# Two cross-attention layers on one core: the plain scores of the second layer read 48 rows each instead of 112

## The chip, the cores and the metric

One of the eight cores of a Trainium2 chip runs the whole program; the others are idle. The time is device microseconds from start to end of one execution, the median of three runs for the kernel before. Engines: TensorE (PE for matmuls, PEld for the loads of its stationary operand), VectorE (DVE), ScalarE (ACT), GpSimd (POOL), and SyncE (SP), which issues most DMAs.

## The reference

Sixteen batches, each with 112 query rows `x` of width 320 and 375 context rows of width 192, go through two attention layers. What matters here, for one batch:

```
# layer 0: 8 heads of width 40; keys are the first 371 context rows
hs  = softmax(q0 k0^T / sqrt(40)) v0            # plus a small attention over 4 extra tokens (ca_hs2)
x1  = (hs + ca_hs2) @ Wout + b_out + x
# layer 1: 20 heads of width 16; keys are all 375 context rows
q = (x1 @ Wq), k = (ctx @ Wk), v = (ctx @ Wv)
s = q k^T / sqrt(16)                            # per head: 112 x 375
out = softmax(s) v @ Wo + bo + x1
```

## The kernel before

Every float32 product that needs accuracy is made of float32r parts: an operand is split into a high part and a low remainder. For layer 1 a head has width 16, and its query is kept three times (high, low, high) in `q1T` and its key three times (low, high, high) in `k1_stack`, so that one contraction over 3 x 16 = 48 rows gives all three partial products. Two heads share a column block: the even head (j = 0) has its 48 rows at partitions 0 to 47, the odd head (j = 1) at partitions 64 to 111. `q1T[:, pair, j, :]` holds the query of head j and zeroes in the other head's rows (line 663 writes the even part, line 826 the odd part with its zeroes, through the factor `odd_rows`).

A softmax needs the row maximum before the exponent. So the scores are computed twice. `scores(g, pair)` computes the plain scores, queries on PSUM's partitions and 376 keys along the columns, for two heads at a time: head j goes to `bankS[:, j]`, which is a PSUM bank of its own. VectorE takes the negative maxima of both heads in one instruction (`maximum`, line 770). `transpose_m` (1162) transposes these maxima, VectorE copies them (776), and a DMA issued by ScalarE places them as a further row of the query (row 48). `shifted_scores` (1177, 1183) then computes the scores again, transposed, with the maximum subtracted, and `attend` (1215) multiplies their exponentials with the values. A group is four heads, so two pairs; layer 1 has five groups per batch, which makes ten pairs per batch and 160 pairs in all, each of two matmuls at line 1149. Layer 0 has its own line, 1146, and is not touched.

The matmuls of `attend`, of line 1115 and of line 987 write only 32 or 64 PSUM partitions each: they run in column tiles, parts of TensorE's array that are used side by side. In the set-up, the last two matmuls of each `query_keys` (line 971) contract over only 64 rows. A float32 matmul shows in the trace as two instructions, a float32r one as one.

The order of the work on each engine is written out by hand. A step t of the loop has seven slots; in a slot TensorE does: first pair of a group, units of phase 0, `shifted_scores` of an older group, `transpose_m`, units of phase 1, second pair, units of phase 2, `attend`, units of phase 3. The units (table `UNITS`) are all the projections and transposes; they share two PSUM banks in turn, so a unit waits until the unit two places before it has been drained by ScalarE or VectorE. Layer 1 is scored in slots 2 to 6. In steady state TensorE goes through the ten pairs of a batch as follows (units in brackets by their name in the table; most of them run at line 995):

- slot 2: [K1_0] **pair 1** [K1_1], shifted scores, maxima, [S3] **pair 2** [N1b, S2_0], attend, [S2_1]
- slot 3: **pair 3** [K1_2], shifted scores, maxima, [K0_0] **pair 4** [hn1T], attend, [K0_1]
- slot 4: **pair 5** [K0_2], shifted scores, maxima, [N0, p3T] **pair 6** [out1], attend, [q0T_0]
- slot 5: **pair 7** [hn0T, V0_0], shifted scores, maxima, [q0T_1] **pair 8** [out0], attend, [T2_0]
- slot 6: **pair 9** [x1T, V0_1], shifted scores, maxima, [T2_1] **pair 10** [q1], attend, [V0_2]

The units hn1T, hn0T, x1T (line 1077), N0, N1a, N1b (1085), q0T (1061) and T2 (1108) are float32 transposes; S3 is line 1123, S2 line 1101, p3T line 1088.

Of the kernel before, what the change touches and what calls it, by code (L numbers as in the profile page):

```python
# [11 lines left out]
B, SQ, HID = 16, 112, 320  # L12
SK, CAD, NTOK = 375, 192, 4
SKE = SK - NTOK
SKP = SK + 1
# [22 lines left out]
M_ROW0, M_ROW1 = 3 * D0, 3 * D1  # L38
ROWS1 = 64 + 3 * D1
# [53 lines left out]
def bank(name, b):  # L93
    return AT[name, b] % 2


def drained(name, b):
    return AT[name, b] // 2 + 1
# [13 lines left out]
def xattn_kernel(nc, xT, xpad, ctxT, caS, caT, w_all, w_ca, wqT, bd96, consts, bias, out):  # L112
    g_rows = nc.dram_tensor("g_rows", [B, 3, 32, HID], F32, kind="Internal").ap()

    with ExitStack() as ctx:
        def sb(name, shape, dt=F32):
            return ctx.enter_context(nc.sbuf_tensor(name, shape, dt))
# [14 lines left out]
        k1_stack = [sb(f"k1_stack{i}", [P, H1 // 2, SKP], F32R) for i in range(2)]  # L132
# [10 lines left out]
        q1T = sb("q1T", [P, H1 // 2, 2, SQ], F32R)  # L143
# [69 lines left out]
        bankS = ctx.enter_context(nc.psum_tensor("bankS", [P, 2, 512], F32))  # L213
# [729 lines left out]
        def _(pe):  # L943
# [183 lines left out]
            def scores(g, pair):  # L1127
                layer, b, k = g
                n = NUMBER[g]
                if n > 0 or pair > 0:  # L1130
                    pe.wait_ge(max_done, 2 * n + pair)
                else:
                    pe.wait_ge(gq_drained, 4)
                if pair == 0 and layer == 0:
                    if k == 0:
                        pe.wait_ge(k0_stacked, 16 * DMAS_K0 * (b + 1))
                    pe.wait_ge(bank_drained[bank(f"q0T_{k}", b)], drained(f"q0T_{k}", b))
                if pair == 0 and layer == 1:
                    if k == 0:
                        pe.wait_ge(k1_stacked[b % 2], 16 * DMAS_K1 * (b // 2 + 1))  # L1140
                        pe.wait_ge(k1_stacked_pool[b % 2], 16 * DMAS_K1 * (b // 2 + 1))
                    pe.wait_ge(bank_drained[bank(f"q1T_{k // 2}", b)], drained(f"q1T_{k // 2}", b))
                for j in range(2):
                    h = GROUP * k + 2 * pair + j
                    if layer == 0:
                        last = nc.tensor.matmul(bankS[0:SQ, j, 0:SKE + 1], q0T[0:M_ROW0, h, :],  # L1146
                                                k0_stack[0:M_ROW0, h, 0:SKE + 1], start=True, stop=True)
                    else:
                        last = nc.tensor.matmul(bankS[0:SQ, j, 0:SKP], q1T[0:ROWS1, h // 2, h % 2, :],  # L1149
                                                k1_stack[b % 2][0:ROWS1, h // 2, :], start=True, stop=True)  # L1150
                last.then_inc(scores_done, 1)

            def transpose_m(g, attended):
# [81 lines left out]
            for t in ITERATIONS:  # L1235
                for i in range(SLOTS):
                    g, before, late = scored_at(t, i), scored_at(t, i, 1), scored_at(t, i, LAG)
                    if g:
                        scores(g, 0)
                    for u in units_of(t, i, 0):  # L1240
                        unit(*u)
                    if late:
                        shifted_scores(late)
                    if before:
                        transpose_m(before, attended)
                        transposed = NUMBER[before] + 1
                    for u in units_of(t, i, 1):
                        unit(*u)
                    if g:
                        scores(g, 1)  # L1250
                    for u in units_of(t, i, 2):
                        unit(*u)
                    if late:
                        attend(late, transposed)
                        attended = NUMBER[late] + 1
                    for u in units_of(t, i, 3):
                        unit(*u)
# [75 lines left out]
```

## Time and profile before

| | |
|---|---|
| median of 3 runs | 777.53 us (777.09 to 777.82) |
| the profiled execution | 777.66 us, of which the span is 775.8 us |
| TensorE matmul busy | 713.3 us, 92% of the span |
| TensorE load busy | 615.3 us, 79% |
| VectorE, ScalarE, GpSimd busy | 61%, 51%, 38% |
| mean granted clock of TensorE | 0.98 of full speed |

Times are microseconds from the start of the span, unless marked ns. A row of the timeline begins with the start and the duration of an instruction or of a run of equal instructions (xN), then engine, source line, operation, the tiles written and read, and the shapes. Behind a matmul's names stand contraction rows * stationary columns, then the moving operand's size: `112*112 112x376` is a contraction of 112 rows, 112 stationary columns and 376 moving columns. A recorded matmul reaches beyond the start of the next one, because matmuls are pipelined and their ends are modelled; the distance from one start to the next is what TensorE spends. A bracket at the end gives idle time before the instruction and what ended it.

### The profile page before, as it was taken

The page shows a single profiled execution, that of the slowest core. Times are in us where ns is not written, and L with a number is a line of the kernel's source. Part 1 is how long each engine was busy: PE and PEld are TensorE (multiplying, and loading weights), DVE is VectorE, ACT ScalarE, POOL GpSimd, SP SyncE. Part 2 cuts the span into 40 slices and gives each one's busy share as a digit, 9 for nine tenths or more (in the row PEclk, how much of TensorE's full clock was granted, in tenths as well). Part 3 has the DMA queues.
Part 4 walks back from the last instruction along what each step waited for, and adds up shares of the span by engine and source line. Part 5 has one row for each costly group of instructions (what it writes and reads, how often), then busy time and mean ns, then how long its engine had stood idle before and what let it go on. Part 6 is the DMA issues. An engine that isn't in the chain of part 4 may idle for free.

```text
span 775.8 us, 18175 instructions
## 1 busy us (share of the span) xinstructions
PE 713.3 (92%) x6916; PEld 615.3 (79%) x6916; DVE 472.7 (61%) x1028; ACT 399.3 (51%) x923; POOL 294.3 (38%) x401
## 2 busy tenths in 40 slices
PE   6978899999899999999999999999999999999985
PEld 5666778888788878888888888888887888888763
DVE  1553565756566575756666575666657565766763
ACT  1445355555455556555555555555555555554432
POOL 5387344333233433332343432333343342330300
PEclk9879899999999999999999999999999999999988
DMA  9433452432715253361815254261725325060400
GB/s 327 140 111 94 96 120 67 89 115 52 146 32 131 79 94 96 66 132 32 170 38 118 75 84 114 49 158 32 145 64 96 93 59 139 2 166 12 84 1 16
DMA packets 52387, 72.45 MB, mean 93 GB/s; under 512 B 12128, under 2 KB 44256, under 8 KB 52304
## 3 DMA queue, kind: packets, MB, share of 16 engines
q1 hardware_dynamic: 44832, 60.34, 32.4%
q0 software_dynamic: 6144, 9.25, 5.9%
q10 hardware_dynamic: 1328, 1.71, 0.6%
q8 instruction: 57, 0.93, 0.5%
q14 instruction: 26, 0.21, 0.1%
HBM read 20.60 MB, written 4.26 MB: 32 GB/s over the span
## 4 chain that ended last, share of the span: by engine, by line
PE 62%; DVE 13%; ACT 7%; DMA 5%; issue 4%; ACTq 2%; POOL 1%; POOLq 0%
PE bankX L995 26%; PE bankO L1215 7%; PE bankST L1183 6%; DMA q1T<-mT 5%; PE bankST L1177 5%; DVE negmax L770 5%; PE bankS L1149 4%; ACT arena L592 3%; DVE q1T L826 2%; PE bankS L1146 2%; PE bankX L1115 2%; PE bankX L1108 2%; ACT q1T L663 2%; PE bankX L1077 2%; PE bankX L1095 1%
## 5 line engine op out<-in xcount | busy, mean ns | idle before, releaser
L770 DVE TENSOR_REDUCE negmax<-bankS 112x2 f32<-112x750 f32 (+1 forms) x224 | 208.6, 931 | 60.9 <-PE bankS L1149 33.4
L494 POOL DMA_DIRECT2D k_stack<-stage x192 | 96.2, 509 | 177.0 <-PE bankST L1177 163.7
L574 ACT ACTIVATE arena<-bankST 125x1344 f32<-125x1344 f32 x80 | 103.5, 1294 | 41.3 <-PE bankST L1183 41.3
L1215 PE MATMUL bankO<-arena,v 125*32 125x112 f32 (+2 forms) x2688 | 107.2, 264 | 6.1 <-ACT arena L574 4.6
L1215 PEld LDWEIGHTS bankO<-arena,v 125*32 125x32 f32 (+2 forms) x2688 | 80.8, 117 | 30.0 <-issue 14.8
L1149 PE MATMUL bankS<-k_stack,q1T 112*112 112x376 f32 x320 | 89.7, 361 | 2.9 <-DVE negmax L770 2.4
L995 PE MATMUL bankX<-ctx_hi,WH 128*120 128x376 f32 (+2 forms) x192 | 71.1, 370 | 13.9 <-ACT arena L592 11.6
L474 POOL TENSOR_TENSOR x1b<-x,bias_sb 112x320 f32<-112x320 f32 x16 | 14.0, 876 | 179.7 <-DMA out<-x1b 155.0
L1183 PE MATMUL bankST<-q1T,k_stack 112*125 112x224 f32 x480 | 67.4, 276 | 5.7 <-DMA q1T<-mT 5.5
L1183 PEld LDWEIGHTS bankST<-q1T,k_stack 112*125 112x125 f32 x480 | 62.5, 191 | 9.4 <-DMA q1T<-mT 9.1
L995 PE MATMUL bankX<-WH,ctx_hi 128*125 128x320 f32 x192 | 66.8, 348 | 0.4 <-ACT q0T L655 0.3
L995 PE MATMUL bankX<-ctx_hi,WL 128*120 128x376 f32 (+2 forms) x192 | 64.9, 338 | 0.0
L995 PE MATMUL bankX<-WL,ctx_hi 128*125 128x320 f32 x192 | 59.2, 316 | 0.0
L776 DVE CAST mT<-bankO 4x112 fp32r<-4x112 f32 x112 | 29.2, 260 | 43.1 <-PE bankO L1162 42.9
L592 ACT ACTIVATE arena<-bankX,negmax 112x112 f32<-112x112 f32 x128 | 43.3, 363 | 23.3 <-DVE negmax L834 23.3
L995 PEld LDWEIGHTS bankX<-ctx_hi,WH 128*120 128x120 f32 (+2 forms) x192 | 35.0, 182 | 25.3 <-ACT arena L592 16.5
L826 DVE TENSOR_SCALAR q1T<-bankX,odd_rows 128x448 fp32r<-128x448 f32 (+1 forms) x48 | 29.1, 606 | 42.3 <-ACT q1T L663 41.8
L1149 PEld LDWEIGHTS bankS<-k_stack,q1T 112*112 112x112 f32 x320 | 49.4, 181 | 6.6 <-DVE negmax L770 4.4
L995 PE MATMUL bankX<-WH,act_hi 128*112 128x320 f32 x144 | 46.4, 322 | 4.9 <-DVE hn L794 3.4
L811 DVE TENSOR_TENSOR stage<-bankX,stage 120x376 fp32r<-120x376 f32 (+1 forms) x48 | 26.2, 545 | 33.9 <-ACT stage L622 33.9
L459 POOL TENSOR_TENSOR w2bd<-w2s,cst 96x896 fp32r<-96x896 f32 x16 | 29.9, 1870 | 42.7 <-DVE w2s L762 42.7
L622 ACT ACTIVATE stage<-bankX 120x376 fp32r<-120x376 f32 (+1 forms) x48 | 23.3, 486 | 44.1 <-PE bankX L995 44.1
(139 smaller groups left out, 1579.9 us busy)
## 6 DMA issues: line engine op xcount, KB each, us to landing
k_stack<-stage SPq DMA_DIRECT2D x96, 176.2 KB
k_stack<-stage SPq DMA_DIRECT2D x192, 70.5 KB, 4.0
k_stack<-stage POOLq DMA_DIRECT2D x192, 47.0 KB, 3.6
ctx_raw<-in_ctxT SPq DMA_DIRECT2D x16, 376.0 KB, 3.0
k_stack<-stage SPq DMA_DIRECT2D x48, 117.5 KB
xp<-in_xpad SPq DMA_DIRECT2D x16, 224.0 KB, 4.2
x_raw<-in_xT SPq DMA_DIRECT2D x16, 168.0 KB, 2.3
out<-x1b SPq DMA_DIRECT2D x16, 140.0 KB, 3.3
```

The lines of the kernel that those rows point to most:

```text
L459: nc.gpsimd.tensor_tensor(w2bd[:, :, :], w2s[:, :].bitcast(F32).unsqueeze(1).broadcast_to((96, H0, SQ)), mask96.unsqueeze(2).broadcast_to( ...
L494: pool.dma_start(dst, src).then_inc(k1_stacked_pool[b % 2], 16)
L574: nc.scalar.activation(dst[0:KC], bankST[0:KC, :, 0:GROUP * SQ], ACT.Exp).then_inc(exp_done, 1)
L592: last = nc.scalar.activation(prob2[0:SQ, h, :], X[0:SQ, (h % 4) * SQ:(h % 4 + 1) * SQ], ACT.Exp, bias=negmax2[:, h:h + 1], accum_out=sum2 ...
L770: nc.vector.tensor_reduce(negmax[:, n % 2, 2 * pair:2 * pair + 2], bankS[0:SQ, :, 0:keys], axis=AX, op=ALU.max, negate=True).then_inc(max_ ...
L776: nc.vector.tensor_copy(mT[:, n % MT_BUFS, :], bank_mT).then_inc(mT_copied, 1)
L826: nc.vector.tensor_scalar(q1T[:, 4 * i:4 * i + g, 1, :], X[:, 0:g * SQ].rearrange("p (h q) -> p h q", h=g), odd_rows[:, :], None, ALU.mult ...
L995: last = nc.tensor.matmul(dst, lhs, rhs, start=(n == 0), stop=(n == len(passes) - 1))
L1149: last = nc.tensor.matmul(bankS[0:SQ, j, 0:SKP], q1T[0:ROWS1, h // 2, h % 2, :], k1_stack[b % 2][0:ROWS1, h // 2, :], start=True, stop=True)
L1177: last = nc.tensor.matmul(bankST[0:keys, c, SQ * j:SQ * j + SQ], k0_stack[0:M_ROW0 + 1, h, KC * c:KC * c + keys], q0T[0:M_ROW0 + 1, h, :], ...
L1183: last = nc.tensor.matmul(bankST[0:KC, c, 2 * SQ * pair:2 * SQ * pair + 2 * SQ], k1_stack[b % 2][0:ROWS1, 2 * k + pair, KC * c:KC * c + KC ...
L1215: last = nc.tensor.matmul(dst, v, src[0:keys, c, SQ * j:SQ * j + SQ], start=(c == 0), stop=(c == NKC - 1))
```

## The change

Each of the two matmuls of a pair at line 1149 contracts only over its own head's 48 rows, which start at partition 64 j, in place of rows 0 to 111. The zero rows of `q1T` are no longer read here (`shifted_scores` still reads them). In the built program, the array tile of these 320 matmuls is 64 rows by 128 columns, at row 0 for j = 0 and at row 64 for j = 1; before it was the whole 128 by 128. Of the other matmuls only sixteen, all in the set-up (lines 954, 971 and 987), use a tile of 64 rows, always at row 0. Nothing is added, removed or put into another order on any engine, and no wait, semaphore, DMA or buffer is different.

```diff
@@ def scores(g, pair): ... for j in range(2): ... layer 1
-                        last = nc.tensor.matmul(bankS[0:SQ, j, 0:SKP], q1T[0:ROWS1, h // 2, h % 2, :],
-                                                k1_stack[b % 2][0:ROWS1, h // 2, :], start=True, stop=True)
+                        rows = slice(64 * j, 64 * j + M_ROW1)
+                        last = nc.tensor.matmul(bankS[0:SQ, j, 0:SKP], q1T[rows, h // 2, j, :],
+                                                k1_stack[b % 2][rows, h // 2, :], start=True, stop=True)
```

`M_ROW1` is 48 and `ROWS1` is 112. In a pair h % 2 is j, so the same query block is read.

## Rows read from the trace of the kernel before

**Rows 1.** The page, part 1.
```profile
PE 713.3 (92%) x6916; PEld 615.3 (79%) x6916; DVE 472.7 (61%) x1028; ACT 399.3 (51%) x923; POOL 294.3 (38%) x401
```

**Rows 2.** A stretch of one batch: us, busy PE PEld DVE ACT POOL, PEclk, DMA.
```profile
400.00:444.40 44.40, 42.77 (x449) 37.40 (x438) 29.07 (x64) 24.76 (x58) 17.62 (x25) 1.00 0.36 92
```

**Rows 3.** The waits of TensorE's weight loads: total us, times, longest.
```profile
PEld bankX L995 <- ACT arena L592: 16.5, 15, 1.1
...
PEld bankST L1183 <- DMA q1T<-mT: 9.1, 13, 1.5
PEld bankX L995 <- DVE hn L794: 8.0, 14, 0.7
...
PEld bankX L995 <- ACT q0T L655: 4.0, 15, 0.6
PEld bankX L1101 <- DVE p L843: 3.8, 13, 0.3
PEld bankX L995 <- ACT arena L671: 3.4, 14, 0.2
```

**Rows 4.** Line 1149 alone: ns minimum/median/maximum of one, first and last start.
```profile
L1149 PE MATMUL bankS<-k_stack,q1T x320: 327/335/656, 91.8 to 759.7; 112*112 112x376 f32 x160
```

**Rows 5.** Timeline of TensorE, a pair in dense work: start, us.
```profile
415.33 0.34 PE L995 MATMUL bankX<-ctx_hi,WL 128*120 128x376 f32 x1
415.51 0.51 PE L1149 MATMUL bankS<-k_stack,q1T 112*112 112x376 f32 x2
415.86 0.33 PE L995 MATMUL bankX<-ctx_hi,WH 128*80 128x376 f32 x1
```

**Rows 6.** Timeline of the set-up: into tiles of 64 rows (matmul, then load).
```profile
22.54 0.54 PE L971 MATMUL bankO<-v,v 128*128 128x192 f32 x2
...
23.01 0.18 PEld L971 LDWEIGHTS bankO<-v,v 64*128 64x128 f32 x1 [0.23 <-issue]
```

**Rows 7.** Timeline of the set-up: back out of them.
```profile
26.70 0.49 PE L971 MATMUL bankS<-v,v 64*128 64x64 f32 x3
27.12 0.40 PE L995 MATMUL bankX<-WH,x_hi 128*112 128x320 f32 x1
27.36 0.31 PE L995 MATMUL bankX<-WL,x_hi 128*112 128x320 f32 x1
```

**Rows 8.** First matmul after column tiles; a transpose after them, and another.
```profile
432.37 0.41 PE L995 MATMUL bankX<-WH,ctx_hi 128*125 128x320 f32 x1
...
400.34 0.32 PE L1085 MATMUL bankX<-cst,o1T 128*112 128x128 f32 x1
...
405.79 0.27 PE L1085 MATMUL bankX<-cst,o1T 128*112 128x128 f32 x1
```

**Rows 9.** The set-up, two matmuls in column tiles: timeline, and the line alone.
```profile
28.47 0.49 PE L987 MATMUL bankST<-v,v 128*64 128x320 f32 x2
...
L987 PE MATMUL bankST<-v,v x14: 432/432/483, 28.5 to 30.4; 128*64 128x320 f32 x14
```

**Rows 10.** Timeline, the loads that wait after pairs 2, 3, 6, 7.
```profile
406.05 0.17 PEld L1101 LDWEIGHTS bankX<-w2bd,ca_st 96*112 96x112 f32 x1 [0.29 <-DVE p L843]
...
409.35 0.19 PEld L995 LDWEIGHTS bankX<-ctx_hi,WH 128*128 128x128 f32 x1 [1.13 <-ACT arena L592]
...
419.11 0.17 PEld L995 LDWEIGHTS bankX<-WH,act_hi 128*112 128x112 f32 x1 [0.56 <-DVE hn L794]
...
422.41 0.18 PEld L995 LDWEIGHTS bankX<-WH,ctx_hi 128*125 128x125 f32 x1 [0.24 <-ACT q0T L655]
```

**Rows 11.** Timeline after pair 4.
```profile
412.86 0.45 PE L1077 MATMUL bankX<-cst,hn 112*128 112x112 f32 x3
413.24 0.41 PE L1215 MATMUL bankO<-arena,v 125*64 125x112 f32 x4
...
412.57 0.54 ACT L571 ACTIVATE arena<-bankST 121x448 f32<-121x448 f32 x1
```

**Rows 12.** Timeline of the end: a pair that waits.
```profile
746.89 0.60 PE L1149 MATMUL bankS<-k_stack,q1T 112*112 112x376 f32 x2 [0.95 <-DVE negmax L770]
```

## The prediction, written before the changed kernel ran

> **What bounds the kernel now.** I read the busy times first: TensorE 92%, the next engine 61% [rows 1]. Then one batch of the steady loop: 42.77 of 44.40 us busy at the full clock, the others at 29.07 and less [rows 2]. So TensorE is the bound for nearly the whole span, and time added between two of its matmuls lengthens the kernel, unless TensorE would have waited soon after for something that was produced before the added time. The waits of its weight loads say where that is: each of five has 13 to 15 cases, once in a batch [rows 3]. Last I read single rows of the timeline, because "busy" hides the price in question: a matmul's record reaches beyond the start of the next.
>
> **The change at one pair.** Nothing is removed in number: 320 matmuls, median 335 ns by their records [rows 4]. In dense work a pair starts at 415.51 and its follower at 415.86 [rows 5], so each matmul holds TensorE for 0.17 us, and a follower starts some 0.16 before the recorded end of the one ahead (0.34 less 0.17). The change does two things.
>
> (a) The two matmuls stand in different halves of the array's rows and write different banks. If the halves work side by side, the pair takes one stream, not two: -0.17 us. No row has two halves by rows at once. The nearest is two matmuls in halves by columns: both lie within 0.49 us, where a single one at that line has a median of 0.43 by its record and at most 0.48 [rows 9], so they share their time. The bounds are therefore -0.17 (side by side) and 0 (one after the other). I take -0.17, since a half by rows differs from one by columns only in which side of the array is cut.
>
> (b) The array goes from whole tiles to 64-row tiles and back. The set-up has just this. The last whole matmul ends by its record at 22.54 + 0.54 = 23.08 us, and the load for the 64-row matmul starts at 23.01 after 0.23 of "issue", in which it waited for nothing the trace shows [rows 6]. It starts 0.07 before that end, where a follower in dense work has its matmul started 0.16 before it: 0.09 us lost. Going back is alike: the last 64-row matmul ends at 26.70 + 0.49 = 27.19, the load and the first matmul start at 27.12, and that matmul has 0.40 against the next one's 0.31 [rows 7]: its load was not hidden, another 0.09. Behind column tiles the first matmul has 0.41 [rows 8], the same. So entering or leaving costs 0.09 + 0.10 = 0.19 us before a float32r matmul of 112 or more stationary columns. Where transposes follow, the unhidden load costs only 0.05 (0.32 against 0.27, [rows 8]), so 0.14.
>
> The pair with a float32r follower: -0.17 + 0.19 + 0.19 = +0.21. With transposes behind it: -0.17 + 0.19 + 0.14 = +0.16. The array's halving saves one stream and pays two switches that each cost more than it.
>
> The Trainium skill, "TensorEngine Tiling (Array Packing)", section Overview, promises up to twice the speed for a contraction of 64 rows or fewer; its section Tiling Modes says that changing the tiling mode drains TensorE. The second agrees with the 0.23 us of "issue" in [rows 6]; by the first alone each dense pair would be 0.17 us shorter.
>
> **Where in a batch it counts.** Ten pairs; five are followed by a wait.
> - Pair 2: the load of S2_0 waits 0.29 for VectorE's line 843 [rows 10], which started from S3, ahead of the pair. The pair has transposes (N1b) behind it and adds at most 0.16. Hidden.
> - Pair 3: K1_2 waits 1.13 for the exponentials of line 592, pair 6: out1 waits 0.56 for line 794 [rows 10]. Hidden.
> - Pair 7: between it and V0_0 stand the hn0T transposes; V0_0's load waits 0.24 for ScalarE's copy 655, which started from q0T_0, ahead of the pair [rows 10]. 0.16 fits in. Pair 9 has the same with T2_0 and line 671: 14 cases of up to 0.2 us [rows 3]. Hidden, but with only 0.08 left.
> - Pair 4: hn1T, then attend. Attend's load is put down to ScalarE's exponential 571, but that ended at 412.57 + 0.54 = 413.11, while attend started at 413.24 [rows 11], after its own switch. So nothing hides this one: +0.16.
> - Pairs 1, 5, 8, 10: float32r matmuls follow at once, no wait before the next product: +0.21 each.
>
> Sum per batch: 4 x 0.21 + 0.16 = 1.00 us. Some 14 of the 16 batches have this pattern (14 cases in most of [rows 3]): +14.0. Against it: TensorE waits 9.1 us in 13 places for the DMA that places the maxima [rows 3]. Two pairs lie between a transposed maximum and its use, so each wait can swallow up to some 0.2 of the delay: about -2.0, with bounds of 0 and -9.1. At the end of the run pairs wait for the maxima with an empty array (0.95 before the pair at 746.89, [rows 12]); there entering costs nothing that was not paid, and the shared stream gives 0.17 each, more at half clock: for some 7 pairs -1.3. The batches at the ends have few dense pairs: 0, at most +1. VectorE gets a dense pair's scores 0.02 later (0.19 more entry, 0.17 less stream), which its 61% bears.
>
> Total: 14.0 - 2.0 - 1.3 = +10.7, or about +11 us on the profiled execution's 777.66, which lies 0.13 above the median of 777.53. Forecast 788.5 us.
>
> **Rivals.**
> 1. The halves don't run side by side: the second matmul follows 0.17 later. Dense pairs then cost 0.38 and 0.33, so a batch 4 x 0.38 + 0.33 = 1.85, and pairs 7 and 9 overrun their 0.24 by 0.09 each: 2.03. Times 14 is 28.4, less some 3 at the DMA waits: about 803. For it: no row shows row halves together. Against: [rows 9].
> 2. The other side: the load for a half is fetched behind the matmul ahead, as in dense work, so a switch costs under 0.085 us, half of the saved stream, which is the point from which it decides; at no price it saves 0.17 at pairs 1, 5, 8, 10 and 0.08 at pair 4, where the exponential then binds (0.13 between 413.11 and 413.24, less the release). 14 x 0.76 = 10.6, with 1.3 at the end: about 765.5. This is the skill's "up to 2x" of the section named above. For it: the 48-row loads are independent. Against: [rows 6, 7] show the stall, in both directions, for the very same tile shape.
> 3. The stall is paid but soaked up: waits of TensorE other than the five, and late DMAs, give back nearly all. Then about 778 to 780. Against: the batch has 1.6 us not busy [rows 2], and most of it sits right behind producers that move along with the delay.
> 4. More is exposed: pairs 7 and 9 not hidden adds 14 x 0.32 = 4.5, giving 793, or with no relief at the DMAs 795.
>
> **Chances.** Forecast 0.62 (own range 785 to 792), rival 4 0.12, rival 1 0.12, rival 3 0.06, rival 2 0.08. The range 782 to 803 takes in the forecast, rival 4 and half of rival 1, a little over 8 in 10. A difference under 0.2% (1.6 us) can't be told from none. Faster is rival 2; "same" is a third to a half of rival 3; the rest is slower: 0.08, 0.03, 0.89.
>
> **What would show it.** In the profile after: line 1149's matmuls as 48*112, the two of a pair starting under 0.02 us apart (rival 1: 0.17). Ahead of each pair's load, and ahead of the follower's, an idle time of about 0.2 us of PEld put down to "issue", some 300 more of them. Start to start from a dense pair's predecessor to its follower 0.74 us (0.53 before, from 415.33 to 415.86, [rows 5]). One batch 45.4 us instead of 44.4. The waits for 655 and 671 shrink to under 0.1, those for 592 by 0.2. VectorE's, ScalarE's and GpSimd's busy times stay. I am wrong if the load of a 64-row tile starts before the matmul ahead has drained, or if a batch stays at 44.4 although the stalls are there.

## The result and the profile after

The changed kernel takes 790.75 us, the median of four runs (787.77 to 792.60), beside 777.67 us for the kernel before: a ratio of 1.0151, 95% interval [1.0118, 1.0184]. A second series later, beside many more runs of the kernel before, gave 788.67 us against 779.57 us, 1.0104 [1.0068, 1.0139]. So the change makes the kernel 1.0% to 1.5% slower, 8 to 13 us. The forecast was 788.5 us, in a range of 782 to 803. In all that follows, a run more than 1.5% above the fastest of its own kernel is left out of median and interval; that happened once, to one run of the last kernel below (794.51 us).

The profiled execution took 791.02 us. Its page, the head, part 1 and the chain by engine, beside [rows 1]:

```profile
span 789.2 us, 18175 instructions
...
PE 728.3 (92%) x6916; PEld 594.6 (75%) x6916; DVE 476.6 (60%) x1028; ACT 399.0 (51%) x923; POOL 294.2 (37%) x401
...
PE 62%; DVE 13%; ACT 7%; DMA 6%; issue 4%; ACTq 2%; POOL 1%; POOLq 0%
```

TensorE's matmul records grew by 15 us, while its load records shrank by 21: two loads now lie over each other and the records count them once. The other engines changed by less than 4 us. A stretch of the steady loop, 44.55 us of it (columns as in [rows 2]):

```profile
400.00:444.55 44.55, 43.15 (x429) 35.64 (x428) 28.77 (x63) 24.30 (x58) 17.07 (x25) 1.00 0.36 91
```

The length of this stretch was chosen as that of a batch of this kernel; the 44.40 us of [rows 2] were an arbitrary stretch and not the length of a batch of the kernel before, which is 43.84 us, as will be seen below. The two rows give busy times and the clock, and nothing of the loss can be read from 44.40 against 44.55.

Line 1149 is line 1150 here. Its own rows, beside [rows 4]: nanoseconds of one matmul, and then TensorE's idle time before this line in us, with the number of cases:

```profile
L1150 PE MATMUL bankS<-k_stack,q1T x320: 393/422/654, 89.8 to 772.1; 48*112 48x376 f32 x160
...
  issue: 16.6, 67
  DVE negmax L770: 5.2, 8
```

A record of 422 ns where there were 335 is the sign of an unhidden load ahead of the stream. What the change did is best seen at one pair. This is pair 1, first in the kernel before:

```profile
401.95 0.33 PE L995 MATMUL bankX<-ctx_hi,WL 128*128 128x376 f32 x1
402.12 0.50 PE L1149 MATMUL bankS<-k_stack,q1T 112*112 112x376 f32 x2
402.46 0.34 PE L995 MATMUL bankX<-ctx_hi,WH 128*128 128x376 f32 x1
```

and in the changed kernel (matmuls, then weight loads):

```profile
403.01 0.34 PE L995 MATMUL bankX<-ctx_hi,WL 128*128 128x376 f32 x1
403.27 0.42 PE L1150 MATMUL bankS<-k_stack,q1T 48*112 48x376 f32 x2
403.63 0.45 PE L995 MATMUL bankX<-ctx_hi,WH 128*128 128x376 f32 x1
...
403.27 0.17 PEld L1150 LDWEIGHTS bankS<-k_stack,q1T 48*112 48x112 f32 x2 [0.24 <-issue]
403.63 0.19 PEld L995 LDWEIGHTS bankX<-ctx_hi,WH 128*128 128x128 f32 x1 [0.18 <-issue]
```

Three things are to be seen. The two matmuls lie within 0.42 us (x2), where one alone would have that record with its load exposed: they stream together. The loads ahead of the pair started after 0.24 us of "issue", and the follower's after 0.18, with no engine named; I read this as the array emptying first. And the follower has 0.45 where its equals have 0.34: its load was not hidden either. From the start of the matmul before the pair to the follower's it takes 403.63 - 403.01 = 0.62 us, and 0.11 more until the follower streams: 0.73. Before, it was 402.46 - 401.95 = 0.51. Pair 1 costs 0.22 us.

TensorE's load waits, beside [rows 3] (total us, cases, longest). The first row is one of the kernel before that [rows 3] leaves out; the others are of the changed kernel:

```profile
PEld bankX L1088 <- DVE stage L811: 6.2, 15, 0.4
...
PEld bankS L1150 <- issue: 16.6, 67, 0.7
PEld bankX L995 <- issue: 16.0, 76, 1.6
PEld bankX L995 <- ACT arena L592: 14.4, 15, 1.0
PEld bankST L1184 <- DMA q1T<-mT: 10.5, 14, 1.6
...
PEld bankX L1077 <- issue: 8.4, 45, 0.3
PEld bankX L995 <- DVE hn L794: 7.0, 15, 0.6
...
PEld bankX L1088 <- DVE stage L811: 3.9, 15, 0.4
...
PEld bankX L995 <- ACT q0T L655: 0.6, 1, 0.6
```

"Issue" is new or larger ahead of the pairs (16.6 us), of line 995 (16.0) and of the transposes at line 1077 (8.4). The waits that followed the hidden pairs shrank, and the one for ScalarE's copy 655 went from 4.0 us in 15 cases to 0.6 in one: the time did not come on top, it took the place of the wait. The same holds for the wait of p3T (line 1088) for VectorE's line 811, which shrank from 6.2 to 3.9 us, 0.15 per case; it stands behind pair 5 and decides below what that pair costs.

The price of the change in the steady loop can be read from the length of a batch. The first matmul of the unit W2 (line 1095) comes once per batch. The kernel before, one batch without a late DMA:

```profile
393.78 0.43 PE L1095 MATMUL bankX<-x_raw,bd 128*96 128x112 f32 x2 [0.25 <-DVE q1T L826]
...
437.62 0.43 PE L1095 MATMUL bankX<-x_raw,bd 128*96 128x112 f32 x2 [0.25 <-DVE q1T L826]
```

The changed kernel, the same batch:

```profile
394.84 0.34 PE L1095 MATMUL bankX<-x_raw,bd 128*96 128x112 f32 x1 [0.26 <-DVE q1T L826]
...
439.39 0.34 PE L1095 MATMUL bankX<-x_raw,bd 128*96 128x112 f32 x1 [0.25 <-DVE q1T L826]
```

That is 43.84 and 44.55 us: +0.71 us per batch. I call such a batch quiet: the shortest ones are 43.82 to 43.88 in three profiles of the kernel before, 44.55 to 44.59 in two of the changed kernel. It is a much finer measure than the time of a run, which moved between 775.33 and 786.58 us for the kernel before alone.

Laid over each other from one W2 to the next, two quiet batches of the two kernels show where the 0.71 us come from. What TensorE does behind pair 1 comes 0.22 us later in the changed kernel. It stays at about 0.2 behind pairs 2 and 3, grows to 0.32 behind pair 4 and to 0.48 behind pair 5, is back at 0.32 from p3T's load on, stays there behind pairs 6 and 7, grows to 0.48 behind pair 8, is 0.48 again behind pair 9, and is 0.70 behind pair 10.

Not every batch is quiet, and this matters for the time of a run. Over twelve batches, from the fourth W2 to the last, the three profiles of the kernel before take 533.5, 533.1 and 535.7 us, the two of the changed kernel 544.0 and 537.4. Twelve quiet batches would be 526.1 and 534.6. What lies above that is 7.0 to 9.6 us before, and 9.4 and 2.8 after; the 9.4 have one special batch, which is the subject of the section on the changed kernel again. Most of it is TensorE's wait for the DMA that places the maxima: 7.2, 6.1 and 7.6 us of it in these batches before, 6.2 and 2.8 after.

### The profile page after: what moved, and what is told of

It is laid out like the page before. It is cut to its first block, busy times and chain, and to the rows that moved or that the text cites. A ratio compares the mean times of both kernels' runs of the same rounds, so it can differ in the third digit from the quotient of the medians.

```text
span 789.2 us, 18175 instructions
## 1 busy us (share of the span) xinstructions
PE 728.3 (92%) x6916; PEld 594.6 (75%) x6916; DVE 476.6 (60%) x1028; ACT 399.0 (51%) x923; POOL 294.2 (37%) x401
## 4 chain that ended last, share of the span: by engine, by line
PE 62%; DVE 13%; ACT 7%; DMA 6%; issue 4%; ACTq 2%; POOL 1%; POOLq 0%
PE bankX L995 26%; PE bankST L1184 7%; PE bankO L1216 7%; DMA q1T<-mT 6%; PE bankST L1178 5%; DVE negmax L770 4%; PE bankS L1150 4%; ACT arena L592 3%; DVE q1T L826 2%; PE bankX L1077 2%; PE bankS L1146 2%; PE bankX L1115 2%; PE bankX L1108 2%; ACT q1T L663 2%; PE bankX L1095 1%
## 5 line engine op out<-in xcount | busy, mean ns | idle before, releaser
L995 PE MATMUL bankX<-ctx_hi,WH 128*120 128x376 f32 (+2 forms) x192 | 73.3, 382 | 12.8 <-ACT arena L592 10.6
L1184 PE MATMUL bankST<-q1T,k_stack 112*125 112x224 f32 x480 | 69.0, 280 | 6.9 <-DMA q1T<-mT 6.8
L1184 PEld LDWEIGHTS bankST<-q1T,k_stack 112*125 112x125 f32 x480 | 63.1, 193 | 11.6 <-DMA q1T<-mT 10.5
L1150 PE MATMUL bankS<-k_stack,q1T 48*112 48x376 f32 x320 | 69.2, 428 | 2.6 <-DVE negmax L770 2.0
L995 PE MATMUL bankX<-WH,act_hi 128*112 128x320 f32 x144 | 50.4, 350 | 4.9 <-DVE hn L794 3.3
L1150 PEld LDWEIGHTS bankS<-k_stack,q1T 48*112 48x112 f32 x320 | 28.1, 172 | 30.4 <-issue 16.6
```

The costliest lines, as they stand in the source:

```text
L995: last = nc.tensor.matmul(dst, lhs, rhs, start=(n == 0), stop=(n == len(passes) - 1))
L1150: last = nc.tensor.matmul(bankS[0:SQ, j, 0:SKP], q1T[rows, h // 2, j, :], k1_stack[b % 2][rows, h // 2, :], start=True, stop=True)
L1184: last = nc.tensor.matmul(bankST[0:KC, c, 2 * SQ * pair:2 * SQ * pair + 2 * SQ], k1_stack[b % 2][0:ROWS1, 2 * k + pair, KC * c:KC * c + KC ...
```

## The experiments

**Both matmuls in the same half.** Same shapes, same switches, no shared stream.

```diff
-                        rows = slice(64 * j, 64 * j + M_ROW1)
-                        last = nc.tensor.matmul(bankS[0:SQ, j, 0:SKP], q1T[rows, h // 2, j, :],
+                        rows = slice(0, M_ROW1)
+                        last = nc.tensor.matmul(bankS[0:SQ, j, 0:SKP], q1T[rows, h // 2, 0, :],
```

> Changed kernel, but both matmuls of a layer-1 pair read rows 0 to 47 (the even head's): same shapes, same two switches, yet the same half of the array, so they can't share a stream. It leaves out the odd heads' plain scores. Theory (two switches of 0.19 us less one shared stream of 0.17): the second matmul starts 0.17 us after the first instead of 0.003, a pair costs 0.38 (0.32 before transposes) more than before where its follower is not waiting, and its result comes 0.18 later instead of 0.02, so pair 5 is no longer hidden: per batch 0.38 x 3 + 0.32 + 0.18 and 0.1 each at pairs 7 and 9 = 1.84 us, about 803 to 806 us. Rival (the halves share nothing worth speaking of, the time comes from the clock or from slower 48-row matmuls): within 1 us of the changed kernel, 790 to 792.

Measured: 806.95 us (803.55 to 810.59), ratio 1.0358 [1.0318, 1.0398], 1 us above the expected range. Its timeline, a pair and its follower (pair 5), and W2 of two batches in a row:

```profile
424.27 0.59 PE L1150 MATMUL bankS<-k_stack,q1T 48*112 48x376 f32 x2
424.79 0.40 PE L995 MATMUL bankX<-ctx_hi,WH 128*80 128x376 f32 x1
...
310.23 0.53 PE L1095 MATMUL bankX<-x_raw,bd 128*96 128x112 f32 x3 [0.26 <-DVE q1T L826]
...
355.92 0.53 PE L1095 MATMUL bankX<-x_raw,bd 128*96 128x112 f32 x3 [0.25 <-DVE q1T L826]
```

The pair's records now reach over 0.59 us instead of 0.42, by 0.17, which is one stream. (The second matmul is recorded 0.26 us after the first, where I had expected 0.17: the first one's record begins with the load that was not hidden, 0.09 us.) A quiet batch is 45.69 us: +1.85 against before, where 1.84 was expected. So in the changed kernel the halves do run side by side, and that saves 1.14 us per batch; without it the change would have cost 29 us, not 8 to 13.

**One matmul in a half tile, the other in the whole array.**

```diff
+                        rows = slice(0, ROWS1) if j == 0 else slice(64, ROWS1)
```

> Kernel before, but only the odd head's matmul of a layer-1 pair reads its own 48 rows at partition 64; the even head's reads all 112. Theory: the switch falls between the two matmuls (0.19) and behind them (0.19 or 0.14), nothing is shared: second start 0.34 to 0.36 us after the first, the dense pairs cost 0.38 and 0.32 more than before as in the run with both in one half, 803 to 806 us. Rival (a smaller share of half tiles means a smaller loss): half of the changed kernel's loss, about 784.

Measured: 808.46 us (806.14 to 811.04), ratio 1.0377 [1.0346, 1.0409], 2.5 us above the expected range; quiet batches of 45.75 to 45.80 us. The second matmul is recorded 0.33 us after the first (median). Half as many half tiles as the changed kernel, but as many switches, and nothing shared: the loss is that of the run above, to within 0.1 us per batch. The number of half tiles is not what costs.

**The four pairs with nothing to hide behind, and the six others.** Batches 0 to 14; the rest keeps 112 rows. The diff is the first's; the other has (2, 3, 5, 6, 7, 9).

```diff
+                        own = b < B - 1 and 2 * k + pair + 1 in (1, 4, 8, 10)
+                        rows = slice(64 * j, 64 * j + M_ROW1) if own else slice(0, ROWS1)
```

> The change at pairs 1, 4, 8 and 10 of a batch alone (batches 0 to 14), 112 rows elsewhere. Theory (the loss is the two switches where no wait follows): from the two traces 0.22 + 0.16 + 0.17 + 0.22 = 0.77 us per batch, 14 to 15 batches: 10.8 to 11.5, plus up to 2 if the clock falls once more: 787.5 to 791. Rival (the loss goes with the number of half-tile pairs, by the granted clock or otherwise): 4 of 10 pairs, so 4/10 of 13.1 = 5 us: 783.

> The change at pairs 2, 3, 5, 6, 7 and 9 of a batch alone (batches 0 to 14): those behind which a wait follows. Theory: 0 to +1 us, 777 to 779, though the same two stalls of 0.19 stand at each of them in the profile. Pair 5, which I had predicted as exposed (+0.21), should be hidden: p3T waits for VectorE's line 811, which stands behind the maximum of pair 5, and that gets its scores only 0.02 later. Rival (the loss goes with the number of half-tile pairs): 6/10 of 13.1 = 8 us: 785.5; had pair 5 been exposed: 780.5.

Measured: pairs 1, 4, 8, 10: 786.21 us (784.67 to 787.99), ratio 1.0092 [1.0064, 1.0120]. The other six: 780.33 us (775.98 to 781.78), ratio 1.0016 [0.9991, 1.0042], no difference that can be told; its median lies 1.3 us above the expected range. W2 of two batches, first in the run with the four:

```profile
216.42 0.43 PE L1095 MATMUL bankX<-x_raw,bd 128*96 128x112 f32 x2 [0.25 <-DVE q1T L826]
...
261.01 0.43 PE L1095 MATMUL bankX<-x_raw,bd 128*96 128x112 f32 x2 [0.26 <-DVE q1T L826]
```

44.59 us, +0.75 per batch, where 0.77 was expected. And in the run with the six, with the idle time put down to "issue" ahead of the pairs:

```profile
394.57 0.53 PE L1095 MATMUL bankX<-x_raw,bd 128*96 128x112 f32 x3 [0.26 <-DVE q1T L826]
...
438.38 0.53 PE L1095 MATMUL bankX<-x_raw,bd 128*96 128x112 f32 x3 [0.26 <-DVE q1T L826]
...
  issue: 8.2, 34
```

43.81 us, as before to within the scatter of quiet batches, although the stalls are there: 8.2 us in 34 cases, half of what the changed kernel has. In a quiet batch six pairs in ten cost nothing and four cost all of it.

The time of the run with the four was a miss. It grew by 8.3 us between the medians, with an interval of 5.0 to 9.3, where I expected 10.8 or more. Its twelve batches take 539.4 us, 5.3 more than the mean of the kernel before, where 0.75 us each would be 9.0. Most of the difference lies in the batches that are not quiet: TensorE waits 4.0 us there for the DMA of the maxima, and 7.0 on average before. So 0.75 us per batch is the price where nothing is late, and the run pays less. Against the rival, whose 5 us lie at the edge of the interval, the batch decides: 4/10 of 0.71 would be 0.28 us.

**Pair 5 and pair 1 alone.** Both have float32r matmuls of the same kind ahead and behind.

```diff
+                        own = b < B - 1 and 2 * k + pair + 1 == 5      # and == 1
```

> The change at pair 5 alone (batches 0 to 14). One look: the time can't tell 1 us, the length of a quiet batch can. Theory: the two stalls stand there, but p3T waits for VectorE's line 811, which stands behind the maximum of pair 5, and that maximum gets its scores only about 0.02 us later: a quiet batch 43.82 to 43.87 us, as before. Rival (my prediction: exposed): 44.06.

> The change at pair 1 alone (batches 0 to 14), which has the same neighbours on TensorE as pair 5, but no such wait behind it: a quiet batch 44.03 to 44.07 us, 0.2 longer than before. Rival (switches are cheaper one by one than ten in a batch): under 43.95.

One run each: 776.71 us and 784.76 us beside 786.58 us for the kernel before, which says only how far single runs scatter. The shortest batches are 43.82 to 43.88 us for pair 5, five of them, and 44.07 and 44.09 for pair 1, two of them, with none shorter from the fourth W2 on. So pair 1 costs 0.23 us and pair 5 nothing. Why, shows in the run with pair 5 alone (from the pair's load to p3T's load):

```profile
415.13 0.17 PEld L1151 LDWEIGHTS bankS<-k_stack,q1T 48*112 48x112 f32 x2 [0.25 <-issue]
415.14 0.42 PE L1151 MATMUL bankS<-k_stack,q1T 48*112 48x376 f32 x2
...
415.24 0.49 ACT L622 ACTIVATE stage<-bankX 120x376 fp32r<-120x376 f32 x1 [1.68 <-PE bankX L995]
...
415.76 0.55 DVE L811 TENSOR_TENSOR stage<-bankX,stage 120x376 fp32r<-120x376 f32 x1 [0.30 <-ACT stage L622]
...
416.23 0.18 DVE L888 TENSOR_TENSOR p3w<-p,p3w 112x32 fp32r<-112x32 f32 x1
...
416.33 0.93 DVE L770 TENSOR_REDUCE negmax<-bankS 112x2 f32<-112x750 f32 x1
...
417.18 0.54 DVE L811 TENSOR_TENSOR stage<-bankX,stage 80x376 fp32r<-80x376 f32 x1
...
417.77 0.12 PEld L1088 LDWEIGHTS bankX<-cst,p3w 112*96 112x96 f32 x1 [0.25 <-DVE stage L811]
```

The chain begins ahead of pair 5. ScalarE's copy at 415.24 (line 622) waited for the unit in front of the pair (K0_1), and VectorE's line 811 waited for that copy. Lines 811 and 888 and the maximum then follow each other without idle time. The maximum of pair 5 starts at 416.33, in its turn behind line 888, and not when the scores are there: by then the pair's records are 0.77 us past their end. Behind the maximum stands the next line 811, at 417.18, and p3T waits for that. From the last matmul ahead of the pair to p3T's load it is 2.90 us here (414.87 to 417.77) and 2.90 in the kernel before (415.33 to 418.23); only the wait in front of that load is shorter, 0.25 in place of 0.41. My expectation had the chain right and its start wrong: the maximum does not even wait for the pair.

**The last batch alone.**

```diff
+                        own = b == B - 1
```

> The change at the ten pairs of the last batch alone (they are computed when little else is left), 112 rows in the other 150. Most of these pairs start after a wait for the maxima, with an empty array, so entering the tile costs nothing new and the shared stream gives 0.16 us at full clock, 0.31 at half. Theory: -1 to -2 us, 776 to 777; I count on no verdict, as this is at the edge of what can be measured. Rival (half tiles pull the clock down at the end, since the last stretch of the changed kernel is 119.8 us after 115.4 and only 1.4 of that is the price at two batches): +2 to +3 us.

Measured: 780.05 us, ratio 1.0003 [0.9976, 1.0029], twelve runs. Neither the gain of 1 to 2 us nor a loss of 2 to 3 is shown; the interval, -1.9 to +2.3 us, holds the smaller half of either.

**The changed kernel again.**

> The changed kernel once more. A quiet batch should again be 44.55 us (43.85 before), which gives 0.7 x 14 to 15 = 10 to 10.5 of the 13.1 us. The rest should be found in stretches at half clock whose place changes from run to run (in the first profile 6.8 us at 613, behind a wait of 1.8 us for a late DMA of the maxima, which made that batch 50.1 us long): if it is in the same place again, it is not chance but the kernel.

Measured: the 788.67 us given above, with a profiled execution of 787.25 us. It has quiet batches of 44.55 to 44.59 us, and no half clock anywhere between 100 and 730 us. The first profile had. There TensorE waited for the DMA of a maximum:

```profile
612.72 0.64 PEld L1184 LDWEIGHTS bankST<-q1T,k_stack 112*125 112x125 f32 x3 [1.65 <-DMA q1T<-mT]
```

and the three stretches from there are (us, busy PE, PEld, DVE, ACT, POOL, then the granted clock):

```profile
606.00:613.00 7.00, 5.62 (x57) 4.23 (x55) 3.57 (x7) 3.21 (x6) 0.00 (x0) 0.99 0.73 193
613.00:619.80 6.80, 6.80 (x47) 5.46 (x47) 1.97 (x4) 2.43 (x3) 4.25 (x7) 0.51 0.08 24
619.80:626.00 6.20, 5.95 (x70) 5.39 (x70) 3.01 (x6) 3.17 (x6) 0.00 (x0) 1.00 0.00 0
```

6.8 us at a granted clock of 0.51, the lower of the two levels of 1.2 and 2.4 GHz. The waiting before it and the slow stretch made this batch 50.1 us long. The second profile has 45.5 us for the same batch, so the event is worth 4.6 us, and it does not come in every run. That is more than the 3.8 us between the two profiled executions; the rest of them differs by small amounts both ways. Why the clock fell here is open. The longest such wait of the second profile, 1.74 us at 734, was followed by 3.4 us at the lower level from 735.3 on; one of 1.61 us at 739 in the first profile and one of 1.46 at 209 in the kernel before had no such fall in the 15 us behind them. And the last kernel below had 10.2 us at the lower level from 141 us on with no wait for a DMA in the 8 us ahead and no wait of its loads above 0.56. Of the fourteen profiles these two, both with 48 rows at every pair, are the only ones whose clock fell between 100 and 730 us, once each. Whether half tiles make that more likely is not tested.

**Pairs directly ahead of attend.** In both kernels the second pair of a group (and its maximum on VectorE) moves behind the units of phase 2, so that attend's column tiles follow. The diff shows TensorE's part; VectorE's is alike.

```diff
-                    if g:
-                        scores(g, 1)
                     for u in units_of(t, i, 2):
                         unit(*u)
+                    if g:
+                        scores(g, 1)
                     if late:
                         attend(late, transposed)
```

> 112 rows, but the second pair of each group (TensorE) and its maximum (VectorE) stand behind the units of phase 2, directly before attend. Base for the next kernel. Nothing is saved; the maxima come 0.4 to 1.3 us later: 778 to 784.

> The same order with 48 rows per matmul. A second pair now leaves its 64-row tiles for attend's column tiles, a switch that TensorE made anyway. Theory: pairs 4, 8 and 10 cost 0.19 - 0.17 = 0.02 instead of 0.16 to 0.22, pair 1 still 0.22, so against the run with 112 rows in this order +0.28 us per batch, +4 us in all. Rival (a half tile costs by itself, wherever it stands, or a change from rows to columns costs more than one switch): +10 us again.

Measured: 782.82 us (ratio 1.0041 [1.0009, 1.0072]) with 112 rows, 786.25 us (1.0082 [1.0050, 1.0115]) with 48: 3.4 us apart, where 4 were expected and 10 by the rival. These times are too coarse to decide, since the intervals overlap. W2 in two successive batches, with 112 rows:

```profile
480.63 0.34 PE L1095 MATMUL bankX<-x_raw,bd 128*96 128x112 f32 x1 [0.24 <-DVE q1T L826]
...
524.74 0.34 PE L1095 MATMUL bankX<-x_raw,bd 128*96 128x112 f32 x1 [0.22 <-DVE q1T L826]
```

and with 48:

```profile
354.34 0.43 PE L1095 MATMUL bankX<-x_raw,bd 128*96 128x112 f32 x2 [0.22 <-DVE q1T L826]
...
398.51 0.43 PE L1095 MATMUL bankX<-x_raw,bd 128*96 128x112 f32 x2 [0.21 <-DVE q1T L826]
```

44.11 against 44.17 us; over all batches the quiet ones are 44.02 to 44.11 and 44.17 to 44.19, so +0.1 for what cost 0.7 in the old order, where 0.28 was expected. Laid over each other, two quiet batches show that each of the five second pairs, directly ahead of attend, changes the delay of what follows by 0.02 us or less. A switch from 64-row tiles to column tiles costs no more than one from the whole array, and TensorE made that one anyway. Pair 1 costs nothing in this order, against the expectation: the unit behind it now waits 0.44 us for VectorE's line 794. The +0.1 stand behind pair 3. Neither version beats the kernel before, because the order itself costs 0.2 us per batch. No kernel here was shown to be faster.

**The kernel before, two more profiles.** Unchanged.

> The kernel before once more, for its profile. It is asked how much the clock's fall in the last stretch differs in an unchanged kernel: in the nine profiles so far the half-clock time behind the last quiet batch is 8 to 36 us, and the last stretch is the longer the more it has. Theory (chance of the run, not the half tiles): between 8 and 25 us here too. Rival (half tiles bring it): 8 to 12 us, as in the first profile of before.

> The same again, a third profile of the kernel before: same expectations. A quiet batch should be 43.82 to 43.88 us in both.

One run each: 776.79 and 781.94 us. The stretch from 660 us to the end in both (columns as above; the first number behind the busy times is the granted clock):

```profile
660.00:775.00 115.00, 97.36 (x1022) 81.56 (x1018) 68.80 (x153) 50.09 (x98) 21.44 (x32) 0.95 0.23 47
```

```profile
660.00:780.10 120.10, 103.63 (x1060) 86.62 (x1048) 70.96 (x156) 50.71 (x101) 22.24 (x34) 0.91 0.21 45
```

115.0 us at a mean clock of 0.95 and 120.1 at 0.91, in the same program. Half-clock time behind 700 us was 11.0, 11.5 and 22.5 us in the three profiles of the kernel before, and 16.0 and 19.5 in the two of the changed one. The rival's 8 to 12 us for the kernel before are refuted by the 22.5. The end of the kernel is a chain of short waits, and how much of it runs at the lower clock changes from run to run; the changed kernel stays within that. In the two slowest experiments, both matmuls in one half and one of them in the whole array, it was 36 and 33 us; whether their longer program or chance did that is open.

## Why the prediction was right, point by point

- **TensorE is the bound.** Right: what was added between its matmuls without a wait behind it came out in full in a quiet batch, 0.75 us at four pairs.
- **The halves share a stream, -0.17.** Right: shown by the run with both in one half, 0.17 in the pair's record and 1.14 us per batch. Rival 1 had this at 803 us; the experiment that imitates it gave 807.
- **A switch costs 0.19, or 0.14 before transposes.** Right, and it could be read from four matmuls in the set-up [rows 6, 7]. Pair 1 costs 0.22 in the timelines of before and after, 0.23 in the run with it alone. Rival 2, in which the loads are fetched ahead, is refuted by 0.24 and 0.18 us of idle time around pair 1, and by 0.18 ahead of nearly every follower. The Trainium skill's page "TensorEngine Tiling (Array Packing)" promises up to twice the speed for a contraction of 64 rows or fewer (Overview), and says that a change of the tiling mode drains TensorE (Tiling Modes). The trace agrees with the first for the stream of the pair alone, 0.42 us where both in one half take 0.59; it agrees with the second in the idle 0.24 and 0.18 us.
- **Pairs 2, 3, 6, 7 and 9 are hidden.** Right: the run with these and pair 5 has the old batch, 43.81 beside 43.84 us.
- **Pair 5 costs 0.21.** Wrong, and the one step of the mechanism that failed. I looked for waits whose producer starts ahead of the pair and found none in TensorE's own order; p3T's wait for line 811 depends on K0_2, which comes after the pair. But VectorE reaches that line late in any case, behind lines 811, 888 and the maximum, a chain that starts from K0_1 ahead of the pair. The other four exposed pairs, 0.79 us by the forecast, came to 0.71 to 0.75. So a quiet batch is 0.71 longer instead of 1.00. The sign "one batch 45.4 us instead of 44.4" used a stretch of 44.40 us that was not a batch: it should have read 44.8 instead of 43.8.
- **The DMA waits soak up 2 us.** Right in direction as far as the profiles show, and rather too small. Over the whole span these waits are 9.1, 9.4 and 9.9 us before, 10.5 and 7.0 after, and say little. But in the twelve batches what lies above quiet batches fell from 7.0 to 9.6 us to 2.8, or to 3.8 in the first profile without its special batch. The other kernels with a longer batch have little of it too: 4.3 us in the run with the four pairs, 3.9 and 2.4 in the two slowest. The run with the six hidden pairs, which has the old batch, has 7.4. Chance has a part in it, since the run with pair 5 alone, whose batch is not longer, has 4.4. So the waits gave back some 3 to 5 us, by an estimate from these sums.
- **The end gives back 1.3 us.** Not shown: the run with the last batch alone has -1.9 to +2.3 us. From the last W2 to the end it takes 115.4, 116.4 and 119.3 us before, 119.9 and 121.4 after, so the end grew by 3 to 4 us on average. Two batches of dense pairs in it would be 1.4; how much of the rest is the clock is open.
- **The sum.** +10.7 was forecast, 13.1 and 9.1 were measured. That the sum lies between is in part luck. Pair 5 was counted too high by 3 us (14 x 0.21), so 14 quiet batches give 9.9 us and not 14.0. The relief at the DMA waits was some 1 to 3 us larger than the 2.0 taken off, and the end, from which 1.3 were taken off, took 3 to 4 more instead. The second profile shows this: of its 8.4 us above the mean of the three profiles of before, the twelve batches are 3.3 (8.5 if all were quiet), the stretch behind them 4.4. In the first profile the fall of the clock at 613 us added some 4.6.
- The signs named in advance came: 48*112, both matmuls at once, 0.2 us of "issue" ahead of the loads, the copy's wait gone. Of the 300 more places with idle "issue" some 200 came: the trace of before has 152 for all weight loads, that of the changed kernel 348. Ahead of the pairs only 67 are listed. Behind lines 1061 and 1108, 56 further pairs have 0.14 to 0.15 us, just under what is listed, and 15 pairs behind line 1123 have 0.04.

## What to carry to other kernels

Filling the half-empty array with a second matmul is worth one stream, and costs two changes of tile shape: 0.17 against 0.38 us here, so a lone pair of 376 columns loses, and one that stands directly ahead of work in column tiles broke even. Before counting a stall, look at what the next instruction waits for, and follow that wait through the other engine's queue, not only back to its producer. Where runs scatter by 1%, the length of one undisturbed period of the loop tells 0.1 us apart. It gives the price of a change where nothing else is late, and not the time of the run: that needs the sum over all periods as well, since waits that come now and then give part of the price back.

## What the runs showed of the hardware that was not expected

- A matmul in 64 rows at row 0 and another in 64 rows at row 64, each into its own PSUM bank, started 0.003 to 0.004 us apart, in all 160 pairs: pair and loads share one stretch of 0.42 and 0.17 us.
- One wait of 1.65 us for a DMA was followed by 6.8 us at a granted clock of 0.51 in one profile; waits of 1.46 and 1.61 us in other places were not, and 10.2 us at the lower level came in another kernel with no such wait ahead.
- The kernel before scattered over 11 us (775.33 to 786.58) in the later series, after 0.8 us in the first four runs. Of the 5.1 us between its second and third profile, the last 116 to 119 us hold 2.9 and twelve batches 2.6.
